# Moving half a chunk of matmuls and the search's constants in a one-core transformer kernel

## The chip, the cores and the metric

The kernel runs on one core of a Trainium2 chip. The metric is the device time of one execution in microseconds, the median of the runs.

## The reference, cut to what matters

`x` has two batch entries of 4096 tokens of width 256. Three stages follow one another: a tokenizer (linear attention with a 4096 x 4096 gate), an attention whose softmax runs over the two batch entries, and a feed-forward for the top half of the tokens, chosen by a router weight. The change touches the attention:

```python
h = tok(x)
mn = layernorm(layernorm(h)) * gamma + beta              # N = 2 entries, L = 4096 tokens
q, k, v = mn @ Wq, mn @ Wk, mn @ Wv                      # 8 heads of 32
g = sigmoid(mn @ Wg + bg)
att = softmax_t(sum over l, c of q[s] * k[t] * scale)    # a 2 x 2 table for each head
o = (sum over t of att[s, t, head] * v[t]) * g
h = h + o @ Wo + bo
h = h + ffn(top half of layernorm(h) by the router weight)
```

## The kernel before, in words

Five engines run instruction streams of their own, in order, and meet on semaphores. Matmuls of float32 data are made of three products of high and low halves (`split_products`). PSUM has eight banks of 128 x 512 float32.

- The tokenizer ends with the Gram sums (L713), which fill banks 0 to 3 in the last chunks.
- `start_mix` (L723) loads the attention's weights, and as soon as TensorE is past the Gram sums it runs the first half, j = 0, of chunk 0's values and gates: `values_and_gates(pr, pe, W2, M, 0, 0)`, 24 matmuls of 128x512 into banks 4 to 7 (V is banks 4 and 5, GB is banks 6 and 7). I write (c, j) for half j of chunk c, so this is (0, 0).
- `head_weights` (L814) makes the 2 x 2 tables. VectorE copies the Gram sums out of banks 0 to 3 (L856). TensorE multiplies them with Wk and Wq (L836, into banks 0 to 2) and VectorE multiplies the results elementwise (L860). TensorE forms the column sums (L845: 32 matmuls of 2 columns, into bank 3) and one more product (L849, into bank 3). Then VectorE and ScalarE make the softmax in small steps (L862 to L877), counted by `hw_step`. The last ones write `att_w`.
- `mix` (L886) walks over eight chunks of 512 tokens of both entries. For each half (c, j), ScalarE scales one value bank by `att_w` (`blend`, L976) and VectorE adds the other (`mixed`, L1020, semaphore `mx_o_ok`). ScalarE takes the sigmoid of the gate banks (L981, `mx_g_ok`), GpSimd multiplies (`gated`, L1120, `mx_og_ok`), ScalarE rounds (`high`, L988) and VectorE makes the low part (`low`, L1026, `mx_ogl_ok`). `project(c, h, s)` (L1158) then multiplies with Wo into banks 0 to 3. TensorE's order is (c, 0), project(c-1, 0), (c, 1), project(c-1, 1). ScalarE's order in chunk 0 is blend(0), high(0), blend(1), high(1), all in order.
- V and GB exist once, so (c, j) waits until the half before it is evacuated (L1177, L1182, L803).
- SyncE issues the loads in the order of the code: after the fourth product (`hw_tp`) the feed-forward's `w1`, `w2` and `b1` (L954 to L957), then chunk 1's four tiles of `halves` (`load_m`, L932, into the other half of a double buffer; semaphore `mx_m_ld1`), then the residual rows (L947).
- GpSimd, in `mix`, waits for `hw_step` 8 (the end of the head weights), then makes the constants for the feed-forward's top-k search (L1089 to L1106: `power`, `ones`, `before`, `index`, `step`, `grid`, `column`, `row`, `not_last`), and only then goes on to `gated`. `power` is first used by `scale` (L1129).

Of the kernel before, what the change touches and what calls it, by code (L numbers as in the profile page):

```python
# [722 lines left out]
def start_mix(pr, W2, heads_in, M, scratch, last_mnT):  # L723


    nc, ins, D, KD, END = pr.nc, pr.ins, pr.D, pr.KD, pr.B * pr.NC
    (ld, made, whi, wlo, m_ld) = (pr.sem(n) for n in ("hw_ld", "hw_made", "hw_hi", "hw_lo", "mx_m_ld0"))
    o_wr = pr.sem("hw_o_wr")
    head = D // pr.H
    block = pr.block  # L730

    @block.sync
    def _(sp):
        sp.wait_ge(pr.sem("ret_done"), END * pr.ST)
        for x in "vg":
            sp.dma_start(heads_in[x][:, :, :], ins[f"attn_W{x}"].rearrange("(k p) n -> p k n", p=P)).then_inc(ld, 16)
        for b in range(2):
            for x in ("hi", "lo"):
                sp.dma_start(M["m_" + x][:, 0, b].bitcast(F32), scratch["mT_" + x][b, 0]).then_inc(m_ld, 16)
        for x in "okq":  # L740
            sp.dma_start(heads_in[x][:, :, 0:D], ins[f"attn_W{x}"].rearrange("(k p) n -> p k n", p=P)).then_inc(ld, 16)
        with nc.allow_non_contiguous_dma(reason="a bias column, once"):
            sp.dma_start(W2["bg_col"][:, :], ins["attn_bg"].rearrange("(k p) -> p k", p=P)).then_inc(ld, 16)
        sp.dma_start(W2["br"][:, :], ins["ffn_br"].partition_broadcast(P)).then_inc(ld, 16)

        sp.wait_ge(pr.sem("mnT_lo_ok"), END * 2)
        for x, tile in zip(("hi", "lo"), last_mnT):
            sp.dma_start(scratch["mT_" + x][pr.B - 1, pr.NC - 1], tile).then_inc(pr.sem("st_mnT"), 16)
        for n, count in (("st_h", 16), ("st_mn", 16), ("st_mnT", 32)):
            sp.wait_ge(pr.sem(n), count * END)  # L750

    @block.gpsimd
    def _(pool):
        pool.wait_ge(pr.sem("ret_done"), END * pr.ST)
        nc.gpsimd.memset(heads_in["same_head"][:, :], 0.0).then_inc(made, 1)
        nc.gpsimd.memset(heads_in["ones"][:, :], 1.0).then_inc(made, 1)
        pool.wait_ge(made, 2)
        for h in range(P // head):
            r = slice(h * head, (h + 1) * head)
            nc.gpsimd.memset(heads_in["same_head"][r, r], 1.0).then_inc(made, 1)  # L760
        pool.wait_ge(made, 2 + P // head)
        pool.wait_ge(ld, 16 * 7)
        pool.wait_ge(pr.sem("wr_ld"), 16)
        for k in range(KD):
            nc.gpsimd.tensor_tensor(heads_in["o_wr"][:, k, :], heads_in["o"][:, k, 0:D], W2["wr"][:, :], ALU.mult).then_inc(o_wr, 1)
        pool.wait_ge(pr.sem("hw_o_sum"), 2)
        nc.gpsimd.tensor_copy(heads_in["o"][:, :, D + 1:D + 2], heads_in["o"][:, :, D:D + 1]).then_inc(o_wr, 1)
        nc.gpsimd.tensor_scalar(W2["sum_wr"][:, :], W2["sum_wr"][:, :], -1.0, None, ALU.mult).then_inc(o_wr, 1)

    @block.scalar  # L770
    def _(act):
        act.wait_ge(ld, 16 * 7)
        for x in "vgo":
            if x == "o":
                act.wait_ge(o_wr, KD + 1)
            nc.scalar.activation(W2[x + "_hi"][:, :, :], heads_in[x][:, :, :], ACT.Copy).then_inc(whi, 1)

    @block.vector
    def _(dve):
        nc.vector.tensor_reduce(W2["sum_wr"][:, :], W2["wr"][:, :], AX_X, ALU.add).then_inc(pr.sem("hw_o_sum"), 1)  # L780
        dve.wait_ge(o_wr, KD)
        nc.vector.tensor_reduce(heads_in["o"][:, :, D], heads_in["o_wr"][:, :, :], AX_X, ALU.add).then_inc(pr.sem("hw_o_sum"), 1)
        for n, x in enumerate("vgo"):
            dve.wait_ge(whi, n + 1)
            nc.vector.tensor_tensor(W2[x + "_lo"][:, :, :], heads_in[x][:, :, :], W2[x + "_hi"][:, :, :].bitcast(F32),
                                    ALU.subtract).then_inc(wlo, 1)

    @block.tensor
    def _(pe):
        pe.wait_ge(m_ld, 64)  # L790
        pe.wait_ge(wlo, 2)
        pe.wait_ge(pr.sem("h_ok"), END * 2)
        pe.wait_ge(pr.sem("mnT_lo_ok"), END * 2)
        values_and_gates(pr, pe, W2, M, 0, 0)


def values_and_gates(pr, pe, W2, M, h, j, gates_free=()):

    cols = slice(j * P, (j + 1) * P)
    vv, gg = pr.sem("mx_vv"), pr.sem("mx_gg")  # L800
    for w, bank, sem, b in (("v", M["V"][1], vv, 1), ("v", M["V"][0], vv, 0), ("g", M["GB"][0], gg, 0),
                            ("g", M["GB"][1], gg, 1)):
        if w == "g" and gates_free:  # L803
            past(pe, pr.sem("mx_g_ok"), gates_free[b])
        i = 0
        for k in range(pr.KD):
            for ww, x in split_products(W2[w + "_hi"][:, k, cols], W2[w + "_lo"][:, k, cols],
                                        M["m_hi"][:, h, b, k, :], M["m_lo"][:, h, b, k, :]):
                i += 1
                mm = pe.matmul(bank[:, :], ww, x, start=i == 1, stop=i == 3 * pr.KD)  # L810
        mm.then_inc(sem, 1)


def head_weights(pr, W2, heads_in, grams, banks):  # L814

    nc, D, KD, B = pr.nc, pr.D, pr.KD, pr.B
    head = D // pr.H
# [10 lines left out]
    def _(pe):  # L828
# [18 lines left out]
        mm.then_inc(col_ok, 1)  # L847
        pe.wait_ge(cols_sb, 1)
        pe.matmul(attp, heads_in["same_head"][:, :], cols[:, :], start=True, stop=True).then_inc(att_ok, 1)  # L849

    @block.vector
    def _(dve):
# [33 lines left out]
def mix(pr, W2, M, products, room, scratch, router, mlp_raw, W3):  # L886
# [1 line left out]

    nc, ins, D, KD, NC = pr.nc, pr.ins, pr.D, pr.KD, pr.NC
    with ExitStack() as ctx:  # L890
        m_hi, m_lo, V, GB = (M[n] for n in ("m_hi", "m_lo", "V", "GB"))
        h_in, rows = (room[n] for n in ("h_in", "rows"))
        base, late = sb(nc, ctx, "base", [P, 2, 2, TPC, D]), sb(nc, ctx, "late", [P, 8 * CH])
        og_hi, og_lo = (sb(nc, ctx, n, [P, 2, 2, KD, CH], F32R) for n in ("og_hi", "og_lo"))
# [66 lines left out]
        def _(act):  # L961
# [8 lines left out]

            def blend(c, j):
                n = c * 4 + 2 * j
                act.wait_ge(vv, n + 2)
                past(act, o_ok, n)
                for s in range(2):
                    nc.scalar.activation(t1[:, s, :], V[1][:, :], ACT.Copy,  # L976
                                         scale=W2["att"][:, s, 1, j:j + 1]).then_inc(t_ok, 1)
                past(act, og_ok, n)
                for s in range(2):
                    act.wait_ge(gg, n + s + 1)  # L980
                    nc.scalar.activation(g_sb[:, s, :], GB[s][:, :], ACT.Sigmoid,  # L981
                                         bias=W2["bg_col"][:, j:j + 1]).then_inc(g_ok, 1)
# [30 lines left out]
        @block.vector  # L1013
        def _(dve):
            def mixed(c, j):
                for s in range(2):
                    n = c * 4 + 2 * j + s
                    past(dve, og_ok, n - 1)
# [63 lines left out]

        @block.gpsimd
        def _(pool):
            pool.wait_ge(pr.sem("hw_step"), 8)
            for n in ("st_mn", "st_mnT"):
                pool.wait_ge(pr.sem(n), (32 if n == "st_mnT" else 16) * pr.B * NC)
            made = pr.sem("mw_made")
            nc.gpsimd.memset(power[:, :], -0.5).then_inc(power_ok, 1)  # L1089
            nc.gpsimd.memset(W3["ones"][:, :], 1.0).then_inc(made, 1)  # L1090
            pool.wait_ge(made, 1)

# [11 lines left out]
            nc.gpsimd.tensor_copy(W3["row"][:, :], W3["index"][:, P:P + 1]).then_inc(made, 1)  # L1104
            pool.wait_ge(made, 6 + 2 * STEPS)
            nc.gpsimd.tensor_scalar(W3["not_last"][:, :], W3["row"][:, :], float(P - 1), None, ALU.is_lt).then_inc(made, 1)  # L1106

            def spread_lanes(c):

# [47 lines left out]
        def _(pe):  # L1157
# [16 lines left out]
            def step(c, h):  # L1174
                if within(c) and c > 0:
                    pe.wait_ge(m_ld[h], c // 2 * 64 + 64)
                    past(pe, o_ok, c * 4)  # L1177
                    values_and_gates(pr, pe, W2, M, h, 0, (c * 4 - 1, c * 4))
                if within(c, 1):
                    project(c - 1, 1 - h, 0)  # L1180
                if within(c):
                    pe.wait_ge(o_ok, c * 4 + 2)  # L1182
                    values_and_gates(pr, pe, W2, M, h, 1, (c * 4 + 1, c * 4 + 2))
                if within(c, 1):
                    project(c - 1, 1 - h, 1)

# [430 lines left out]
def build(nc, ins, out, batches, tokens, width, heads, hidden):  # L1617
# [3 lines left out]
    with ExitStack() as ctx:  # L1621
# [36 lines left out]
                   "w1": work[:, n:2 * n].rearrange("p (k n) -> p k n", k=KD)}  # L1658
        with ExitStack() as phase:
            halves = sb(nc, phase, "halves", [P, 4 * KD * hidden], F32R)  # L1660
            M = {"V": banks[4:6], "GB": banks[6:8]}
            M["m_hi"], M["m_lo"] = (halves[:, i * 2 * n:(i + 1) * 2 * n].rearrange(
                "p (h b k t) -> p h b k t", h=2, b=2, k=KD) for i in range(2))
            W2["bg_col"], W2["att"] = sb(nc, phase, "bg_col", [P, KD]), sb(nc, phase, "att_w", [P, 2, 2, KD])
# [2 lines left out]
            with ExitStack() as heads_phase:  # L1667
# [3 lines left out]
                     ("att", [P, 2, 2, 2]), ("top", [P, 2, 2]), ("shifted", [P, 2, 2, 2]), ("expd", [P, 2, 2, 2]),  # L1671
                     ("total", [P, 2, 2]), ("inv", [P, 2, 2])])}
                start_mix(pr, W2, heads_in, M, scratch, pr.last_mnT)
                head_weights(pr, W2, heads_in, gram_view(work, width), banks[0:4])
            products = psum[:, 0:TPC * CH].rearrange("p (j n) -> p j n", j=TPC)
            mix(pr, W2, M, products, room, scratch, router, mlp_raw, W3)
        mlp(pr, W2, W3, ident, scratch, router)
# [38 lines left out]
```

## Time and profile before

| | us |
|---|---|
| median of 3 runs | 2070.14 (2069.56 to 2070.2) |
| the profiled execution | 2072.95 |
| its span | 2071.2 |
| TensorE busy | 1988.7 (96%) |
| VectorE, ScalarE, GpSimd busy | 1222.2, 675.0, 451.0 |

The profiled execution took 2072.95 us, of which 2071.2 are the span that the trace covers; the remaining 1.75 us lie around it. It is 2.81 us over the median of the other runs. All rows and all clock times below are of this execution, in us from the start of its span. A matmul's duration in a row is its latency. Neighbours overlap, so the pace of a stretch is read from the starts.

### The profile page before, as it was taken

To read this page: it belongs to the slowest core of one execution; us is meant where nothing else is said; L and a number is where in the kernel's file an instruction comes from. 1 tells how busy PE (TensorE), PEld (TensorE's weight loads), DVE (VectorE), ACT (ScalarE), POOL (GpSimd) and SP (SyncE) were. 2 spreads that over 40 slices of the span, in tenths; PEclk is the share of its full clock that TensorE was granted. 3 is DMA by queue.
4 is the path that set the end of the run, shared out by engine and by line. 5 is a ranking of instruction groups with operands and counts; after the bars stand their busy time and mean duration, and the time that the engine had idled before them with its cause. 6 is when DMAs were issued, how large, how long until landed. Compare 5 with 4: busy or idle time off the path is not lost.

```text
span 2071.2 us, 27479 instructions
## 1 busy us (share of the span) xinstructions
PE 1988.7 (96%) x9534; PEld 1646.7 (80%) x9534; DVE 1222.2 (59%) x2220; ACT 675.0 (33%) x1093; POOL 451.0 (22%) x578
## 2 busy tenths in 40 slices
PE   7999999999999999999999999999999989829998
PEld 6888888888888888888888888888887878718897
DVE  4656565665656556656565665656554358756553
ACT  4422222222222225422222222222222147524454
POOL 3302020202202023312020201202023057532342
PEclk9999999999999999999999999999999989959999
DMA  4232433334243333242433334243334469620110
GB/s 143 88 105 73 162 112 122 112 122 145 75 164 112 122 112 132 72 153 81 154 112 123 111 122 150 73 162 112 112 112 143 148 241 313 220 77 22 42 42 31
DMA packets 88114, 250.14 MB, mean 121 GB/s; under 512 B 11968, under 2 KB 32448, under 8 KB 88000
## 3 DMA queue, kind: packets, MB, share of 16 engines
q1 hardware_dynamic: 84928, 240.27, 34.5%
q0 software_dynamic: 3072, 8.44, 1.3%
q8 instruction: 61, 1.00, 0.2%
q14 instruction: 53, 0.43, 0.1%
HBM read 194.05 MB, written 54.62 MB: 120 GB/s over the span
## 4 chain that ended last, share of the span: by engine, by line
PE 90%; DVE 4%; issue 2%; ACT 2%; POOL 1%; DMA 0%; SPq 0%; DVEq 0%; ACTq 0%; POOLq 0%
PE bank L663 34%; PE bank L678 34%; PE bank L1568 4%; PE bank L810 4%; PE bank L1588 4%; PE bank L713 3%; PE bank L1169 2%; PE bank L635 1%; PE bank L609 1%; PE bank L619 1%; DVE kt L482 0%; DVE vf L493 0%; PE bank L648 0%; ACT work L380 0%; PE bank L836 0%
## 5 line engine op out<-in xcount | busy, mean ns | idle before, releaser
L678 PE MATMUL bank<-x_hi,kt 128*128 128x512 f32 x2048 | 724.0, 395 | 1.5 <-DVE work L519 1.4
L519 DVE SCALAR_TENSOR_TENSOR work<-bank,d_col,gate 128x512 f32<-128x512 f32 x512 | 383.8, 750 | 553.7 <-PE bank L678 544.7
L398 ACT ACTIVATE p_hi<-work 128x512 fp32r<-128x512 f32 x512 | 324.1, 633 | 1065.5 <-PE bank L663 1024.9
L678 PEld LDWEIGHTS bank<-x_hi,kt 128*128 128x128 f32 x2048 | 384.4, 188 | 90.4 <-DVE work L519 2.4
L663 PE MATMUL bank<-p_hi,v_hi 128*128 128x512 f32 x1024 | 407.0, 397 | 0.3 <-ACT yT L360 0.2
L663 PE MATMUL bank<-p_hi,v_lo 128*128 128x512 f32 x1024 | 404.2, 395 | 0.0
L663 PE MATMUL bank<-p_lo,v_hi 128*128 128x512 f32 x1024 | 403.4, 394 | 0.0
L678 PE MATMUL bank<-x_lo,kt 128*128 128x512 f32 x1024 | 401.0, 392 | 0.0
L507 DVE TENSOR_TENSOR p_lo<-work,p_hi 128x512 fp32r<-128x512 f32 x512 | 367.4, 718 | 29.3 <-ACT p_hi L398 29.2
L568 POOL TENSOR_SCALAR spread<-mv 128x4 f32<-128x4 f32 x16 | 4.9, 308 | 1125.4 <-DVE mv L451 1125.4
L663 PEld LDWEIGHTS bank<-p_hi,v_hi 128*128 128x128 f32 x1024 | 192.2, 188 | 50.6 <-DVE p_lo L507 5.3
L663 PEld LDWEIGHTS bank<-p_hi,v_lo 128*128 128x128 f32 x1024 | 192.3, 188 | 46.3
L663 PEld LDWEIGHTS bank<-p_lo,v_hi 128*128 128x128 f32 x1024 | 193.2, 189 | 44.7
L678 PEld LDWEIGHTS bank<-x_lo,kt 128*128 128x128 f32 x1024 | 192.3, 188 | 43.4
L1534 DVE TENSOR_TENSOR act_lo<-act,act_hi 128x512 fp32r<-128x512 f32 x64 | 59.2, 925 | 91.0 <-ACT act_hi L1472 90.8
L1568 PE MATMUL bank<-ffn,act_hi 128*128 128x256 f32 x512 | 97.4, 289 | 0.0
L1588 PE MATMUL bank<-fx_hi,ffn 128*128 128x512 f32 x256 | 92.5, 408 | 2.2 <-DVE fx_lo L1483 2.2
L1568 PEld LDWEIGHTS bank<-ffn,act_hi 128*128 128x128 f32 x512 | 84.2, 194 | 4.3 <-DVE act_lo L1534 0.2
L575 POOL TENSOR_TENSOR mn_sb<-mn_sb,gamma 128x256 f32<-128x256 f32 x64 | 55.2, 893 | 98.7 <-DVE mn_sb L456 98.7
L1568 PE MATMUL bank<-ffn,act_lo 128*128 128x256 f32 x256 | 73.6, 288 | 0.0
L713 PE MATMUL bank<-kt 128*128 128x256 f32 (+1 forms) x384 | 68.3, 339 | 2.2 <-DVE kt L544 2.2
L713 PEld LDWEIGHTS bank<-kt 128*128 128x128 f32 x384 | 59.2, 189 | 11.2 <-DVE kt L544 2.9
(226 smaller groups left out, 2271.7 us busy)
## 6 DMA issues: line engine op xcount, KB each, us to landing
gate<-in_gateT SPq DMA_DIRECT2D x256, 512.0 KB, 3.6
work<-in_xT SPq DMA_DIRECT2D x32, 512.0 KB, 4.7
scratch_rows<-rows SPq DMA_DIRECT2D x16, 518.0 KB, 4.0
scratch_h<-work SPq DMA_DIRECT2D x16, 512.0 KB, 3.0
scratch_mn<-mn_sb SPq DMA_DIRECT2D x16, 512.0 KB, 6.8
scratch_mT_hi<-mT_hi SPq DMA_DIRECT2D x16, 512.0 KB, 2.7
scratch_mT_lo<-mT_lo SPq DMA_DIRECT2D x16, 512.0 KB, 4.0
gate<-scratch_mn SPq DMA_DIRECT2D x16, 512.0 KB, 4.2
```

What stands on the lines that cost most here:

```text
L398: nc.scalar.activation(p_hi[:, i % 2, :], p32[:, i % RP, :], ACT.Copy).then_inc(hi_done, 1)
L507: nc.vector.tensor_tensor(p_lo[:, i % 2, :], p32[:, i % RP, :], p_hi[:, i % 2, :].bitcast(F32), ALU.subtract).then_inc(lo_done, 1)
L519: nc.vector.scalar_tensor_tensor(p32[:, i % RP, :], S[i % 2][:, :], d_col[:, i:i + 1], gate[:, g % RG, j, :], ALU.add, ALU.mult).then_inc( ...
L575: nc.gpsimd.tensor_tensor(mn_sb[:, j, :], mn_sb[:, j, :], W["gamma"][:, :], ALU.mult).then_inc(scaled, 1)
L663: mm = pe.matmul(Y[m][:, :], v, p, start=i == 0 and n == 0, stop=i == ST - 1 and n == 2)
L678: mm = pe.matmul(S[i % 2][:, :], w, x, start=n == 1, stop=n == 3 * KD)
L713: mm = pe.matmul(out, w, x, start=early(c, 1) and j == 0 and n == 0, stop=False, skip_group_check=True)
L810: mm = pe.matmul(bank[:, :], ww, x, start=i == 1, stop=i == 3 * pr.KD)
L1169: mm = pe.matmul(products[:, j, 0:D + 2], x, w, start=i == 0, stop=i == 3 * KD - 1)
L1534: nc.vector.tensor_tensor(a_lo[:, j % 2, :], act32[:, j % 2, :], a_hi[:, j % 2, :].bitcast(F32), ALU.subtract).then_inc(al_ok, 1)
L1568: mm = pe.matmul(YB[t // 2][:, (t % 2) * D:(t % 2 + 1) * D], a, w, start=j == 0 and t % 2 == 0 and n == 0, stop=j == FT - 1 and n == 2, sk ...
L1588: mm = pe.matmul(HB[j % 2][:, :], w, x, start=n == 1, stop=n == 3 * KD)
```

## The change

The second half of chunk 0, (0, 1), gets four banks of its own: V_first is banks 1 and 0, GB_first is banks 2 and 3, and `blend` and `mixed` read from there (`mix_banks`). TensorE runs it at the end of `head_weights`, right behind the column sums and the product of L849; the matmuls into bank 3 wait for `hw_step` 1, VectorE's copy of that bank. Chunk 0 drops out of TensorE's loop in `mix`. (1, 0), which goes to banks 4 to 7, now waits for `mx_o_ok` 2 and the gates 1 and 2 only, the evacuation of (0, 0).

GpSimd makes the search's constants once the Gram sums are done (`g_done`) and the tokenizer's stores have left, and waits for `hw_step` 8 behind them. `power` is set after that wait.

```diff
+def mix_banks(M, c, j):
+    return (M["V_first"], M["GB_first"]) if (c, j) == (0, 1) else (M["V"], M["GB"])
...
-def values_and_gates(pr, pe, W2, M, h, j, gates_free=()):
+def values_and_gates(pr, pe, W2, M, c, h, j, gates_free=()):
+    V, GB = mix_banks(M, c, j)
...
+    for w, bank, sem, b in (("v", V[1], vv, 1), ("v", V[0], vv, 0), ("g", GB[0], gg, 0), ("g", GB[1], gg, 1)):
+        if (c, j) == (0, 1) and w == "g" and b == 1:
+            pe.wait_ge(pr.sem("hw_step"), 1)
...
         pe.matmul(attp, heads_in["same_head"][:, :], cols[:, :], start=True, stop=True).then_inc(att_ok, 1)
+        values_and_gates(pr, pe, W2, M, 0, 0, 1)
...
         def _(pool):
-            pool.wait_ge(pr.sem("hw_step"), 8)
             for n in ("st_mn", "st_mnT"):
                 pool.wait_ge(pr.sem(n), (32 if n == "st_mnT" else 16) * pr.B * NC)
+            pool.wait_ge(pr.sem("g_done"), NC)
             made = pr.sem("mw_made")
-            nc.gpsimd.memset(power[:, :], -0.5).then_inc(power_ok, 1)
...
             nc.gpsimd.tensor_scalar(W3["not_last"][:, :], W3["row"][:, :], float(P - 1), None, ALU.is_lt).then_inc(made, 1)
+            pool.wait_ge(pr.sem("hw_step"), 8)
+            nc.gpsimd.memset(power[:, :], -0.5).then_inc(power_ok, 1)
...
                 if within(c) and c > 0:
                     pe.wait_ge(m_ld[h], c // 2 * 64 + 64)
-                    past(pe, o_ok, c * 4)
-                    values_and_gates(pr, pe, W2, M, h, 0, (c * 4 - 1, c * 4))
+                    if c == 1:
+                        pe.wait_ge(o_ok, 2)
+                        values_and_gates(pr, pe, W2, M, c, h, 0, (1, 2))
+                    else:
+                        pe.wait_ge(o_ok, c * 4)
+                        values_and_gates(pr, pe, W2, M, c, h, 0, (c * 4 - 1, c * 4))
...
-                if within(c):
+                if within(c) and c > 0:
                     pe.wait_ge(o_ok, c * 4 + 2)
...
+            M = {"V": banks[4:6], "GB": banks[6:8], "V_first": [banks[1], banks[0]], "GB_first": banks[2:4]}
```

## Rows read from the trace of the kernel before

**Rows 1.** The page: TensorE's busy time, and the last chain by engine.
```profile
PE 1988.7 (96%) x9534; PEld 1646.7 (80%) x9534; DVE 1222.2 (59%) x2220; ACT 675.0 (33%) x1093; POOL 451.0 (22%) x578
...
PE 90%; DVE 4%; issue 2%; ACT 2%; POOL 1%; DMA 0%; SPq 0%; DVEq 0%; ACTq 0%; POOLq 0%
```
**Rows 2.** Who waited for whom, TensorE: us in total, times, the longest.
```profile
PE bank L810 <- DVE late L1020: 7.6, 2, 4.0
```
**Rows 3.** Timeline, TensorE: start, length, instruction, idle before it and its releaser.
```profile
1645.02 0.63 PE L810 MATMUL bank<-halves,wv_hi 128*128 128x512 f32 x2
...
1650.62 1.89 PE L836 MATMUL bank<-hw_k,work 128*128 128x256 f32 x8
...
1662.33 0.61 PE L849 MATMUL bank<-hw_cols,hw_same_head 128*128 128x16 f32 x2 [0.27 <-DVE hw_cols L862]
1666.99 1.22 PE L810 MATMUL bank<-halves,wv_hi 128*128 128x512 f32 x2 [4.05 <-DVE late L1020]
...
1677.82 1.19 PE L810 MATMUL bank<-halves,wv_hi 128*128 128x512 f32 x2 [3.51 <-DVE late L1020]
...
1686.25 0.28 PE L1169 MATMUL bank<-wo_hi,og_hi 128*128 128x258 f32 x1
...
1689.11 0.62 PE L810 MATMUL bank<-halves,wv_hi 128*128 128x512 f32 x2
```
**Rows 4.** Stretches of this stage: length, busy times, granted clock, DMA share, GB/s.
```profile
1657.50:1662.30 4.80, 4.57 (x33) 4.46 (x31) 0.86 (x2) 0.00 (x0) 0.00 (x0) 0.76 0.65 232
1662.30:1667.00 4.70, 0.62 (x3) 0.51 (x3) 2.54 (x10) 2.49 (x4) 2.19 (x7) 0.50 1.10 330
1667.00:1670.40 3.40, 3.40 (x8) 2.71 (x9) 0.00 (x0) 1.53 (x3) 3.21 (x6) 0.52 1.02 412
1670.40:1674.20 3.80, 3.80 (x17) 2.82 (x15) 0.00 (x0) 0.48 (x1) 3.72 (x7) 1.00 0.78 312
...
1677.80:1683.50 5.70, 5.68 (x13) 4.44 (x14) 2.39 (x2) 1.55 (x4) 3.64 (x3) 0.50 1.00 400
1683.50:1686.20 2.70, 2.70 (x12) 2.19 (x11) 1.41 (x2) 1.77 (x3) 0.23 (x1) 0.92 0.08 30
```
**Rows 5.** Timeline, ScalarE, of the first chunk of the mix.
```profile
1664.70 1.26 ACT L976 ACTIVATE late<-bank,att_w 128x512 f32<-128x512 f32 x2 [0.85 <-DVE att_w L877]
...
1667.28 1.27 ACT L981 ACTIVATE late<-bank,bg_col 128x512 f32<-128x512 f32 x2
...
1675.50 1.25 ACT L976 ACTIVATE late<-bank,att_w 128x512 f32<-128x512 f32 x2
```
**Rows 6.** Timeline, GpSimd: constants from 1664.59 to 1672.4, then the gated products.
```profile
1664.59 0.11 POOL L1089 MEMSET power<- 128x4 f32 x1 [23.57 <-DVE att_w L877]
...
1672.21 0.23 POOL L1106 TENSOR_SCALAR not_last<-row 128x1 f32<-128x1 f32 x1
1672.40 2.53 POOL L1120 TENSOR_TENSOR late<-late 128x512 f32<-128x512 f32 x2
```
**Rows 7.** Timeline, VectorE: the Gram sums' copies, and chunk 0's second low parts.
```profile
1645.22 1.95 DVE L856 COPY work<-bank 128x512 f32<-128x512 f32 x4 [3.45 <-PE bank L713]
...
1679.45 2.54 DVE L1026 TENSOR_TENSOR og_lo<-late,og_hi 128x512 fp32r<-128x512 f32 x2 [1.78 <-ACT og_hi L988]
```
**Rows 8.** Timeline, SyncE's queue: the first and last of chunk 1's four loads.
```profile
1659.29 3.42 SPq L932 DMA_DIRECT2D halves<-scratch_mT_hi  x1
...
1663.97 0.48 SPq L932 DMA_DIRECT2D halves<-scratch_mT_lo  x1
```
**Rows 9.** DMA issues, of the last of these: size, us from issue to landing.
```profile
halves<-scratch_mT_lo SPq DMA_DIRECT2D x1, 512.0 KB, 7.7
```
**Rows 10.** Stretches elsewhere (columns of rows 4): tokenizer, and the feed-forward's first unit.
```profile
70.00:75.00 5.00, 4.24 (x18) 2.93 (x17) 4.93 (x8) 3.18 (x7) 4.09 (x8) 1.00 0.35 105
...
1860.00:1865.00 5.00, 2.88 (x10) 1.97 (x8) 4.49 (x8) 3.26 (x6) 2.85 (x2) 0.84 0.18 53
1865.00:1870.00 5.00, 4.35 (x17) 4.07 (x18) 2.55 (x9) 1.12 (x2) 0.00 (x0) 0.50 0.02 3
```

More of the change, by code:

```diff
@@ L793, in _ @@
         pe.wait_ge(pr.sem("mnT_lo_ok"), END * 2)
-        values_and_gates(pr, pe, W2, M, 0, 0)
-def values_and_gates(pr, pe, W2, M, h, j, gates_free=()):
+        values_and_gates(pr, pe, W2, M, 0, 0, 0)
+def mix_banks(M, c, j):
+    return (M["V_first"], M["GB_first"]) if (c, j) == (0, 1) else (M["V"], M["GB"])
+def values_and_gates(pr, pe, W2, M, c, h, j, gates_free=()):
+    V, GB = mix_banks(M, c, j)
     cols = slice(j * P, (j + 1) * P)
     vv, gg = pr.sem("mx_vv"), pr.sem("mx_gg")
-    for w, bank, sem, b in (("v", M["V"][1], vv, 1), ("v", M["V"][0], vv, 0), ("g", M["GB"][0], gg, 0),
-                            ("g", M["GB"][1], gg, 1)):
+    for w, bank, sem, b in (("v", V[1], vv, 1), ("v", V[0], vv, 0), ("g", GB[0], gg, 0), ("g", GB[1], gg, 1)):
+        if (c, j) == (0, 1) and w == "g" and b == 1:
+            pe.wait_ge(pr.sem("hw_step"), 1)
         if w == "g" and gates_free:
@@ L811, in values_and_gates, with head_weights @@
         mm.then_inc(sem, 1)
-def head_weights(pr, W2, heads_in, grams, banks):
+def head_weights(pr, W2, heads_in, grams, banks, M):
     nc, D, KD, B = pr.nc, pr.D, pr.KD, pr.B
@@ L890, in mix @@
     with ExitStack() as ctx:
-        m_hi, m_lo, V, GB = (M[n] for n in ("m_hi", "m_lo", "V", "GB"))
+        m_hi, m_lo = M["m_hi"], M["m_lo"]
         h_in, rows = (room[n] for n in ("h_in", "rows"))
@@ L972, in blend @@
                 n = c * 4 + 2 * j
+                V, GB = mix_banks(M, c, j)
                 act.wait_ge(vv, n + 2)
@@ L1015, in mixed @@
             def mixed(c, j):
+                V, _ = mix_banks(M, c, j)
                 for s in range(2):
@@ L1176, in step @@
                     pe.wait_ge(m_ld[h], c // 2 * 64 + 64)
-                    past(pe, o_ok, c * 4)
-                    values_and_gates(pr, pe, W2, M, h, 0, (c * 4 - 1, c * 4))
+                    if c == 1:
[4 more added lines that the diff above has]
+                        values_and_gates(pr, pe, W2, M, c, h, 0, (c * 4 - 1, c * 4))
                 if within(c, 1):
                     project(c - 1, 1 - h, 0)
-                if within(c):
+                if within(c) and c > 0:
                     pe.wait_ge(o_ok, c * 4 + 2)
-                    values_and_gates(pr, pe, W2, M, h, 1, (c * 4 + 1, c * 4 + 2))
+                    values_and_gates(pr, pe, W2, M, c, h, 1, (c * 4 + 1, c * 4 + 2))
                 if within(c, 1):
@@ L1660, in build @@
             halves = sb(nc, phase, "halves", [P, 4 * KD * hidden], F32R)
-            M = {"V": banks[4:6], "GB": banks[6:8]}
+            M = {"V": banks[4:6], "GB": banks[6:8], "V_first": [banks[1], banks[0]], "GB_first": banks[2:4]}
             M["m_hi"], M["m_lo"] = (halves[:, i * 2 * n:(i + 1) * 2 * n].rearrange(
@@ L1673, in build @@
                 start_mix(pr, W2, heads_in, M, scratch, pr.last_mnT)
-                head_weights(pr, W2, heads_in, gram_view(work, width), banks[0:4])
+                head_weights(pr, W2, heads_in, gram_view(work, width), banks[0:4], M)
             products = psum[:, 0:TPC * CH].rearrange("p (j n) -> p j n", j=TPC)
```

## The prediction

> **What bounds the kernel now.** I read the page first. TensorE is busy for 96% of the span, and the chain that ended last lies on it for 90% [rows 1]. A change can gain only where TensorE stands still or runs slowly, so I next asked for whom it waited. The reader should see two waits of the values and gates (L810) for the mix of the half before, 7.6 us together, the longest 4.0 [rows 2]. TensorE's timeline gives their places. After the head weights' last product, which ends at 1662.94, it idles 4.05 us and starts (0, 1) at 1666.99; it idles again for 3.51 us and starts (1, 0) at 1677.82. It reaches project(0, 0) at 1686.25, and from there on it does not stop in this stage [rows 3].
>
> The stretches show a second loss. The granted clock is 1.00 (2.4 GHz) up to the column sums, falls to 0.50 (1.2 GHz) while they run, and stays there until some 3.4 us into (0, 1). After the second idle time it is 0.50 once more, for 5.7 us of (1, 0) [rows 4]. (0, 0), the same 24 matmuls at full clock, took 1650.62 - 1645.02 = 5.60 us. (0, 1) took from 1666.99 to 1677.82 - 3.51 = 1674.31, which is 7.32 us, and (1, 0) took 1686.25 - 1677.82 = 8.43 us [rows 3].
>
> **The change, part by part.** The landmark is the start of project(0, 0), 1686.25 now. What lies before 1662.94 keeps its order on TensorE.
>
> (0, 1) starts at about 1662.95 instead of 1666.99. It no longer waits for the mix of (0, 0); what it adds is a wait for `hw_step` 1, VectorE's 0.2 us copy right behind the last product. That wait stands before the 19th matmul, so I cost it at nothing. If the copy were late, (1, 0) would queue behind it. The start falls into a stretch at 0.50, so I take the durations of the two halves that also started low: 7.32 us, or 8.43 us as the other end. (0, 1) then ends at 1670.3 or at 1671.4.
>
> (1, 0) is queued next. Its banks are free early: the mix of (0, 0) is done by 1666.9, when it releases TensorE now [rows 3], and the two sigmoids end at 1667.28 + 1.27 = 1668.55 [rows 5]. What is late next is the data. Chunk 1's loads stand in SyncE's queue behind the two big feed-forward weights. The last is issued at 1663.97 and lands 7.7 us later, at 1671.7 [rows 8, 9]. Before, there were 6 us of slack on it and nobody waited. Neither the order nor the release of these DMAs changes, since they wait for `hw_tp` alone. So (1, 0) starts at 1671.8 for either end of (0, 1), and a new idle time of 0.4 to 1.5 us stands before it.
>
> How long (1, 0) then takes is the largest unknown. The clock should have risen during (0, 1), as it did about 3.4 us after the earlier resume, and a short pause need not undo it. In the tokenizer a stretch with 0.76 us idle kept 1.00. In the feed-forward's first unit a stretch with 2.12 us idle was followed by one at 0.50 [rows 10]. The new pause lies between. I take 5.60 us, the full-clock row, because the pause is nearer to the first row for most of its range; the bound is 8.43 us, the whole of the slow row. (1, 0) ends at 1677.4, at worst at 1680.2.
>
> **GpSimd's part.** Chunk 0 of the mix is a chain in which ScalarE rounds (0, 0) before it blends (0, 1), and it can round only when GpSimd has multiplied. GpSimd does so at 1672.40, not because of the gate, ready at about 1667.95, but because its constants fill 1664.59 to 1672.4 [rows 5, 6]. After the change these 7.8 us lie behind the Gram sums, which VectorE begins to copy at 1645.22 [rows 7]; so they run from about 1645.3 to 1653.1, beside the copies and the elementwise products. If they doubled the copies' 1.95 us, these would end at 1649.1, still before the products at 1650.62 [rows 3, 7]: cover of 3.4 us, and I cost it at nothing. Setting `power` late costs 0.11 us, and its first reader comes after chunk 0.
>
> The multiplications then start at 1668.0, 4.4 us earlier, and the chain moves with them. The blend of (0, 1) moves from 1675.50 to 1671.1, after its value banks (first 12 of its matmuls, at most 12/24 of a low half of 10.3 us, so by 1668.1). The first low part of (0, 1), now ready at 1679.45 + 0.7 = 1680.1, is ready at 1675.7. Project(0, 0) needs this and TensorE's turn: it starts at max(1675.7, 1677.4) = 1677.4. Without GpSimd's part it would be 1680.1, so that part is worth up to 2.7 us.
>
> Behind it, (1, 1) wants to start 2.86 us later, at 1680.3 (1689.11 - 1686.25 [rows 3]), and needs the mix of (1, 0). ScalarE is free for that at 1676.3, and the mix takes about 2.2 us, from the blend's start at 1664.70 to 1666.9 [rows 3, 5], so it is ready between 1678.5 and 1679.2. One microsecond of slack is left, and TensorE is again the bound, as now. SyncE's load of chunk 2 is released by the gates of (0, 1), earlier too, and has until 1688.7.
>
> **The sum.** 1686.25 - 1677.4 = 8.85 us gained: 4.04 from (0, 1)'s earlier start, 3.51 - 0.1 from the second wait, 2.83 from the clock in (1, 0), less about 1.4 for the new wait for data. Everything behind is a chain on TensorE and the search, which should move as a block. The profiled time 2072.95 becomes 2064.1. It lies 2.81 over the median, and 2070.14 - 8.85 gives 2061.3.
>
> **A transfer that is slower.** In the sum the four tiles land at 1671.7 because the queues moved 412 GB/s from 1667.0 to 1670.4. The stretch before shows 330 [rows 4]. If the last 4.7 us of the transfer ran at that pace, 1.94 MB would take 5.9 us and land at 1672.9; (1, 0) would end at 1678.5, and the time would be 2062.5. Here the Trainium skill weighs against my number: its page "SBUF — State Buffer", section "Summary: rules for kernel authors", says to plan HBM loads at about 358 GB/s. By that figure the landing is an estimate of 1672.4 and the time 2062.0. The trace shows 412 sustained for such a load, and the measurement decides.
>
> **Rivals.**
> 1. The clock. The pause before (1, 0), or the slow start, leaves the clock at 0.50 for a good part of (1, 0). For it speaks the feed-forward's row; against it, the shortness of the pause. The price is up to 2.83 us: 2062.5 to 2064.1. Chance 0.22.
> 2. The late transfer, 2062.5 and somewhat more if the weights' traffic is in its way as well: chance 0.08.
> 3. The gain is larger. All that follows starts 8.85 us earlier, and the clock need not rise and fall at the same instructions. In the feed-forward's first unit it is low for about 6.6 us between 1860 and 1870 and a little after [rows 10]; without that fall up to 3.4 us more are saved. That gives 2058 to 2060.5. Chance 0.12.
> 4. The gain is given back in the mix or at its end, by a wait for stores or loads that had hidden behind the old pauses. I see none: chunk 2's loads get 17 us. It would give 2068 to 2072. Chance 0.04.
> 5. Slower, by one mechanism: the clock that fell in the column sums does not rise. At 1.2 GHz a half takes 10.3 us, so (0, 1) ends at 1673.2 and (1, 0) at 1683.5, still 2.8 us early. Project(0, 0) costs 2.3 more and (1, 1) 4.7 more, and at its end the kernel is 4.1 us behind: 2074.3. It decides from about 1688 on; TensorE would have to run low through 25 us of dense matmuls, where the longest such start seen here took 5.7 us [rows 4]. Chance 0.03.
> The rest, 0.51, is the forecast.
>
> **How the numbers follow.** About 0.2%, or 4.1 us, is what a measurement of this kernel can tell from no change. The forecast and rivals 1 to 3 all end faster than 2066.0: 0.93. Rival 4 is same, 0.04, and rival 5 slower, 0.03. The range takes in rivals 1 and 2 above and most of rival 3 below: 2058.5 to 2064.6.
>
> **What the profile would show.** TensorE should go from L849 into L810 with no idle time, at 1662.95, and wait once, up to 1.5 us, for a DMA of `halves` at about 1671.8. GpSimd's constants should lie at 1645 to 1653, its first L1120 near 1668.0, and project(0, 0) near 1677.4. The copies of L856 should end before 1650. The prediction is wrong if (1, 0) shows 0.50, if its data lands at another time, or if project(0, 0) waits for a low part after 1677.4.

## The result, and the profile after

The changed kernel takes 2065.94 us in the median, the kernel before 2071.07 us in the runs beside it; the ratio is 0.9974, with a 95% interval of 0.9965 to 0.9983. The interval leaves out 1: it is faster, by some 5.4 us (3.5 to 7.2). I had forecast 8.85 us and 2061.3, with a range up to 2064.6: the direction is right, the size and the range are not. One of the changed kernel's twelve executions took 4401.3 us, for a reason that nothing here shows, and the ratio leaves it out. Two further timings of the same kernel (e3 and e10 below) gave 0.9968 (0.9956 to 0.998) and 0.9967 (0.9955 to 0.9979), 6.6 and 6.8 us.

The profiled execution tells another story at first sight. Its span is 2062.0 us, 9.2 less than the 2071.2 of the one before. Lines have moved: L818 is now the values and gates (L810 before), L857 the last product of the head weights (L849), L1182 `project` (L1169), L1133 the gated product (L1120). This is TensorE's timeline, as in [rows 3]: start, length, instruction, idle time before it.

```profile
1645.27 0.63 PE L818 MATMUL bank<-halves,wv_hi 128*128 128x512 f32 x2
...
1661.97 0.61 PE L857 MATMUL bank<-hw_cols,hw_same_head 128*128 128x16 f32 x2 [0.27 <-DVE hw_cols L871]
1662.42 1.20 PE L818 MATMUL bank<-halves,wv_hi 128*128 128x512 f32 x2
...
1672.43 0.73 PE L818 MATMUL bank<-halves,wv_hi 128*128 128x512 f32 x2 [1.73 <-DMA halves<-scratch_mT_lo]
...
1678.13 0.28 PE L1182 MATMUL bank<-wo_hi,og_hi 128*128 128x258 f32 x1
```

The two waits for VectorE's share of the mix are gone. (0, 1) follows the last product without a pause, and one new wait of 1.73 us stands before (1, 0), for chunk 1's data. The stretches, as in [rows 4] (length, busy times by engine, granted clock, DMA share, GB/s):

```profile
1662.40:1667.60 5.20, 5.20 (x13) 4.13 (x14) 2.56 (x10) 3.43 (x6) 0.10 (x1) 0.50 1.09 336
1667.60:1672.40 4.80, 3.10 (x13) 2.12 (x11) 2.50 (x4) 3.28 (x7) 2.55 (x2) 0.98 1.02 410
1672.40:1678.10 5.70, 5.67 (x24) 4.60 (x25) 3.75 (x6) 3.89 (x7) 3.98 (x3) 1.00 1.03 410
```

The clock is 0.50 for the first 5.2 us of (0, 1), rises within it and holds over the pause, so (1, 0) takes 5.70 us. GpSimd's timeline, as in [rows 6]:

```profile
1645.59 0.21 POOL L1100 MEMSET ones<- 128x128 bf16 x1 [4.32 <-PE bank L713]
...
1653.18 0.23 POOL L1116 TENSOR_SCALAR not_last<-row 128x1 f32<-128x1 f32 x1
...
1667.76 2.55 POOL L1133 TENSOR_TENSOR late<-late 128x512 f32<-128x512 f32 x2 [3.43 <-ACT late L991]
```

The constants lie behind the Gram sums, and the first gated product starts at 1667.76 instead of 1672.40. On VectorE, as in [rows 7], the copies of the Gram sums take 1.95 us beside the constants, exactly as without them, and the low parts of (0, 1) start 4.6 us earlier:

```profile
1645.47 1.95 DVE L865 COPY work<-bank 128x512 f32<-128x512 f32 x4 [3.46 <-PE bank L713]
...
1674.86 2.54 DVE L1037 TENSOR_TENSOR og_lo<-late,og_hi 128x512 fp32r<-128x512 f32 x2 [1.80 <-ACT og_hi L998]
```

**A yardstick.** (0, 0) starts at 1645.02 in one profile and at 1645.27 in the other, and between 1644.41 and 1647.73 over all profiles of this study, though nothing ahead of it was changed. So I compare the stage, from the start of (0, 0) to the start of project(0, 0). It took 41.23 us before [rows 3] and takes 1678.13 - 1645.27 = 32.86 us: 8.4 us gained where the timing says 5 to 7. The experiments had to explain both what each half of the change does and where the 2 us went.

### The profile page after: what moved, and what is told of

It is laid out like the page before. It is cut to its first block, busy times and chain, and to the rows that moved or that the text cites. A ratio compares the mean times of both kernels' runs of the same rounds, so it can differ in the third digit from the quotient of the medians.

```text
span 2062.0 us, 27479 instructions
## 1 busy us (share of the span) xinstructions
PE 1985.3 (96%) x9534; PEld 1643.8 (80%) x9534; DVE 1222.6 (59%) x2220; ACT 675.0 (33%) x1093; POOL 453.0 (22%) x578
## 4 chain that ended last, share of the span: by engine, by line
PE 92%; DVE 3%; issue 2%; DMA 1%; ACT 1%; SPq 1%; POOL 0%; DVEq 0%; ACTq 0%; POOLq 0%
PE bank L663 35%; PE bank L678 34%; PE bank L1585 4%; PE bank L818 4%; PE bank L1605 4%; PE bank L713 3%; PE bank L1182 2%; PE bank L635 2%; PE bank L648 1%; PE bank L619 1%; PE bank L609 1%; DMA halves<-scratch_mT_lo 0%; PE bank L844 0%; PE bank L1574 0%; DVE top_counts L1278 0%
## 5 line engine op out<-in xcount | busy, mean ns | idle before, releaser
L519 DVE SCALAR_TENSOR_TENSOR work<-bank,d_col,gate 128x512 f32<-128x512 f32 x512 | 383.9, 750 | 553.4 <-PE bank L678 544.0
```

The source lines that it names most:

```text
L519: nc.vector.scalar_tensor_tensor(p32[:, i % RP, :], S[i % 2][:, :], d_col[:, i:i + 1], gate[:, g % RG, j, :], ALU.add, ALU.mult).then_inc( ...
```

## The experiments

Where a ratio is given, the kernel was timed beside the kernel before; e4, e7, e8 and e12 are one profiled execution each. The diffs are against the kernel named. A gain in us is the ratio's distance from 1, taken of the median before; the stage is that of the one profile.

**e1, GpSimd's half alone** (against the kernel before):

```diff
         def _(pool):
-            pool.wait_ge(pr.sem("hw_step"), 8)
...
+            pool.wait_ge(pr.sem("g_done"), NC)
             made = pr.sem("mw_made")
-            nc.gpsimd.memset(power[:, :], -0.5).then_inc(power_ok, 1)
...
+            pool.wait_ge(pr.sem("hw_step"), 8)
+            nc.gpsimd.memset(power[:, :], -0.5).then_inc(power_ok, 1)
```

> GpSimd's half of the change alone: the constants are made behind the Gram sums, the second half of chunk 0 stays in the shared banks and in its old place. Theory A (the stage works as I costed it): (0, 1) still starts at 1667, but the multiplications start 4.4 us earlier, the wait before (1, 0) shrinks from 3.5 us to nothing, (1, 0) starts at about 1674.3 and runs at full clock, 5.6 us: project(0, 0) at about 1679.9 and some 6 us gained, more than the whole change gained in the timed runs (5.1). Theory B (in ordinary runs the clock is high anyway, and the profiled execution of before was an unlucky one): only the 3.5 us of waiting go, about 3.5 us gained or less.

Measured: 2065.61 us, ratio 0.9976 (0.9965 to 0.9986), 5 us. The stage took 33.60 us. TensorE waits for the mix only once in it (timeline):

```profile
1665.82 1.22 PE L810 MATMUL bank<-halves,wv_hi 128*128 128x512 f32 x2 [4.05 <-DVE late L1020]
...
1672.97 0.63 PE L810 MATMUL bank<-halves,wv_hi 128*128 128x512 f32 x2
...
1678.57 0.28 PE L1170 MATMUL bank<-wo_hi,og_hi 128*128 128x258 f32 x1
```

(0, 1) takes 7.15 us, and (1, 0) follows with no pause and takes 5.60. The interval, 2.9 to 7.2 us, holds both theory A's 6 us and theory B's 3.5; the profile decides between them, and it shows A's course. The 4.4 us by which GpSimd is earlier clear the second wait and the clock loss behind it. Of theory B, one half comes back below: the first profile of the kernel before was an unlucky one.

**e2, the banks' half alone** (against the changed kernel: GpSimd's edit above undone).

> The banks' half alone: (0, 1) runs behind the column sums in banks of its own, the constants stay where they were. By the working of the prediction project(0, 0) then waits for the low part of (0, 1), ready at 1680.1: 6.1 us gained against before, 2 us behind the whole change. If instead the data of chunk 1 sets the end of this stage, it is as fast as the whole change (project(0, 0) near 1678).

Measured: 2066.54 us, ratio 0.9978 (0.9969 to 0.9987), 4.6 us. The stage took 34.47 us. TensorE's wait for chunk 1's data, and the row of project(0, 0):

```profile
PE bank L818 <- DMA halves<-scratch_mT_lo: 2.8, 1, 2.8
```

```profile
1682.20 0.39 PE L1180 MATMUL bank<-wo_hi,og_hi 128*128 128x258 f32 x1 [0.24 <-DVE og_lo L1037]
```

So that project did wait for its low part, as I had worked out. The idle time is short, 0.24 us, only because (1, 0) ended late as well: it waited 2.79 us for its data, and behind this pause it took 7.41 us. An earlier (1, 0) would have gained nothing: the low part's instruction started at 1681.05 and took 1.10 us, to 1682.15, that is 34.4 us behind (0, 0), where I had worked out 35.1. In this version GpSimd's late constants set the end of the stage. Against the changed kernel beside it (e3) it is 2.9 us slower in the median and 1.7 us in the stage; I had expected 2. Either half of the change alone gains most of what both gain.

**e3 and e4, both kernels again**, unaltered.

> The changed kernel unaltered, for a second profiled execution and more timed runs on the chip of the others. Theory A (the gain in the stage is 8 us in every execution, and part of it is lost elsewhere): from the start of (0, 0) to project(0, 0) it takes 32.9 us as in the first profile, and the rest of the span varies. Theory B (the stage itself differs from run to run with the clock): this stretch is 1.5 to 3 us longer. Timed: 0.9974 of before again, 5 us.

> The kernel before, unaltered, for a second profiled execution. Theory A: from (0, 0) to project(0, 0) 41.2 us again, span within 2 us of 2071.2. Theory B: in this stretch the clock comes back earlier or does not fall before (1, 0), and it takes 38.5 to 40 us, a span near 2068.

Measured: the changed kernel 2063.68 us, ratio 0.9968 (0.9956 to 0.998), its stage 32.78 us, as e3's theory A has it (e10 below will differ). The kernel before gave 2071.03 us with a span of 2069.3, and its stage took 39.50 us instead of 41.23: (1, 0) took 7.20 us instead of 8.43, and the way from (0, 0) to (0, 1) 0.5 us less. The distance from (0, 1) to (1, 0), 10.84 us, is unchanged; what moved is when the clock came back. The start of (1, 0) in its timeline:

```profile
1678.17 0.89 PE L810 MATMUL bank<-halves,wv_hi 128*128 128x512 f32 x2 [3.02 <-DVE late L1020]
```

**e7, e8 and e12, the kernel before three more times**, to learn how the first profile stands among others.

> The kernel before, unaltered, for a third profiled execution. The first two took 41.23 and 39.50 us from (0, 0) to project(0, 0), with a mean granted clock of 0.977 and 0.978. Theory B: with a mean clock of 0.981 this stretch is 38 to 38.7 us (the 2.8 us of (1, 0) are not lost at all); with 0.977 to 0.978 it is 39.5 to 41.3. Theory A: 39.5 to 41.3 with any mean clock.

> As the run before this one: a fourth profiled execution of the kernel before, with the same two expectations.

> A fifth profiled execution of the kernel before. The four so far took 41.23, 39.50, 39.63 and 38.71 us from (0, 0) to project(0, 0), with 8.43, 7.20, 7.22 and 7.02 us for (1, 0). If the first was the exception: 38.7 to 39.7 us again.

| kernel before | stage | (0, 0) to (0, 1) | (0, 1) to (1, 0) | (1, 0) | behind it |
|---|---|---|---|---|---|
| first profile | 41.23 | 21.97 | 10.83 | 8.43 | 384.95 |
| e4 | 39.50 | 21.46 | 10.84 | 7.20 | 383.93 |
| e7 | 39.63 | 21.58 | 10.83 | 7.22 | 383.74 |
| e8 | 38.71 | 20.86 | 10.83 | 7.02 | 383.48 |
| e12 | 38.91 | 20.85 | 10.84 | 7.22 | 383.77 |

The first profile was the exception, as e12's text has it: it is the longest in every column that varies at all. The mean stage is 39.60 us. Theory A, 39.5 us or more in every execution, falls with e8 and e12. Theory B is right that the loss differs between executions (its 38 to 38.7 us met 38.71 and 38.91) and wrong on how: it expected no clock loss in (1, 0) in the good ones, and all five show one. Their shortest (1, 0), 7.02 us, is still 1.4 over the full-clock 5.6. The other varying column is the way to (0, 1), and there the column sums. In e8 the clock held through them and fell only in the pause behind; the stretches of e8:

```profile
1656.90:1661.20 4.30, 4.03 (x35) 3.84 (x33) 0.87 (x2) 0.00 (x0) 0.00 (x0) 1.00 0.68 224
1661.20:1665.20 4.00, 0.01 (x1) 0.00 (x0) 2.54 (x10) 2.42 (x4) 2.12 (x7) 0.60 1.10 319
...
1676.10:1679.00 2.90, 2.90 (x7) 2.32 (x8) 1.12 (x2) 1.34 (x3) 2.90 (x3) 0.50 1.01 386
1679.00:1683.10 4.10, 4.10 (x18) 3.32 (x18) 2.68 (x3) 1.96 (x3) 0.97 (x2) 0.99 0.78 313
```

In e8 the low level lasts 2.9 us into (1, 0), where the first profile has 5.7 [rows 4].

**e6, the clock held up in the second pause** (against the kernel before; 14 matmuls more, whose result nobody reads):

```diff
                     pe.wait_ge(m_ld[h], c // 2 * 64 + 64)
+                    if c == 1:
+                        for i in range(14):
+                            pe.matmul(products[:, 0, :], W2["v_hi"][:, 0, 0:P], m_hi[:, 1, 0, 0, :], start=True, stop=True)
                     past(pe, o_ok, c * 4)
```

> The kernel before, with 14 additional matmuls of 512 columns, whose result nobody reads, in TensorE's pause before (1, 0); the waits stay. Theory B (the kernel before loses a different amount in each execution because the clock falls in this pause in some and not in others): (1, 0) takes 5.6 us in every execution, the median falls by 1 to 2.8 us below 2070.9 and the slowest executions (2072 to 2074) are gone. Theory A (the stage is the same in every execution, and the clock costs the same 2.8 us each time): 2.8 us or more gained in all executions, the spread stays. If the clock does not matter: no change, or slower by what the matmuls run over the end of the pause.

Measured: 2068.69 us beside 2071.3, ratio 0.9989 (0.998 to 0.9998). The runs spread over 3.8 us (2067.01 to 2070.78); those of before over 5.3 (2069.33 to 2074.64). The stretches of the pause and of (1, 0):

```profile
1674.30:1677.80 3.50, 3.44 (x15) 2.45 (x14) 3.15 (x4) 2.89 (x6) 0.94 (x2) 1.00 0.66 227
1677.80:1683.50 5.70, 5.70 (x24) 4.60 (x25) 3.72 (x4) 3.38 (x6) 4.01 (x4) 1.00 1.02 407
```

With the waits left in place and TensorE kept busy, the clock stays at 1.00 and (1, 0) takes 5.70 us, 1.7 less than the mean of the five profiles (7.42). The median gained is 2.3 us with an interval of 0.4 to 4.1. So the clock in (1, 0) was worth about 1.7 us in an ordinary execution, not the 2.83 of my sum. The two profiles that reached (0, 1) as early as this one, e8 and e12 (20.86 and 20.85 us, here 20.85), put it at 1.3 to 1.5. That the slowest runs are gone fits a price that varies with it, but eleven runs do not prove it.

**e5 and e11, chunk 1's data earlier** (against the changed kernel):

```diff
             def step(c, h):
-                if within(c, -1):
+                if within(c, -1) and c > 0:
                     load_m(c + 1, 1 - h)
...
+            sp.wait_ge(pr.sem("g_done"), NC)
+            load_m(1, 1)
             sp.wait_ge(pr.sem("hw_tp"), 4)
             sp.dma_start(mlp_raw["w1"], ins["ffn_w1"].rearrange("(k p) n -> p k n", p=P)).then_inc(raw_ld, 16)
```

> The changed kernel with chunk 1's four loads issued as soon as the Gram sums are done (about 1645.5) instead of behind the feed-forward's weights (1659.5). Theory A (the new wait of 1.7 us for this data is on the path): (1, 0) starts where (0, 1) ends, 1670.7, ends at 1676.3, and project(0, 0) starts there, 0.8 us behind its low part: 1.7 us faster than the changed kernel, from (0, 0) to project(0, 0) about 31.1 us. Rival (another wait stands right behind, or the clock falls less often with the pause gone or more often): under 0.7 us.

> The changed kernel with early loads, again, beside the changed kernel on one chip: 31.1 us from (0, 0) to project(0, 0), and 1.7 us faster than the changed kernel; ratio to before 0.9955 to 0.9963.

Measured: 2062.65 us, ratio 0.9952 (0.9939 to 0.9966), and 2062.69 us, ratio 0.9957 (0.9943 to 0.997); beside e11 the changed kernel (e10) took 2064.79. The stage takes 31.09 and 31.54 us. This is the fastest version, 8.9 to 9.9 us under the kernel before. Of TensorE's waits in this stage e5 keeps only the 0.3 us for VectorE's copy of the column sums, which every version has; e11 has this one besides:

```profile
PE bank L1184 <- DVE og_lo L1039: 0.5, 1, 0.5
```

Between e11 and the changed kernel beside it lie 2.1 us in the median. The mean stages, 31.3 us here and 33.24 over the three profiles of the changed kernel, differ by 1.9, where 1.7 was expected. The wait for data was on the path. Now e11's project(0, 0) waits 0.5 us for its low part, so the evacuation through ScalarE and GpSimd is the next bound.

**e9, GpSimd's half with early data, without the banks** (both edits shown above, on the kernel before).

> GpSimd's half of the change with chunk 1's loads issued behind the Gram sums, without the banks' half. Theory C (without the banks (1, 0) starts only when (0, 1) ends, after its data has landed, so the loads are not on the path): from (0, 0) to project(0, 0) 33.6 us as in GpSimd's half alone, same time within 1 us. The banks are then worth 0.8 us with late data and 2.5 us with early data. Rival: the loads matter here too (they take the traffic off the first chunk's evacuation), 1 us or more faster than GpSimd's half alone.

Measured: 2065.76 us, ratio 0.9973 (0.9962 to 0.9985), as e1. The stage took 34.75 us, 1.15 more than e1's, but all of that lies ahead of (0, 1), in the column sums (22.15 us from (0, 0) to (0, 1), where e1 had 20.85). From (0, 1) to project(0, 0) it is 12.60 us, and 12.75 in e1. So theory C holds: without the banks the loads are not on the path. With the data early, the banks are worth 3.1 us in the median (e11's 2062.69, timed beside this 2065.76).

**e10, the changed kernel a third time.**

> The changed kernel unaltered, on the chip and against the runs of the others of this call. From (0, 0) to project(0, 0) 32.8 us; if the gain of the stage is 7 us in the mean, the ratio lies at 0.9966 to 0.9971. If the first timing (0.9974, 5 us) is the truth, 2 us of the stage's gain are lost elsewhere and it comes out there again.

Measured: 2064.79 us, ratio 0.9967 (0.9955 to 0.9979). But the stage took 34.08 us instead of the 32.8 expected, and this profile shows rival 1 at work. The wait for the data (2.81 us here, as (0, 1) had run faster) and the stretches of (0, 1), of the pause and of the start of (1, 0):

```profile
1674.15 0.73 PE L818 MATMUL bank<-halves,wv_hi 128*128 128x512 f32 x2 [2.81 <-DMA halves<-scratch_mT_lo]
```

```profile
1663.90:1671.30 7.40, 7.40 (x26) 5.63 (x25) 2.58 (x11) 4.66 (x7) 2.10 (x3) 0.77 1.06 353
1671.30:1674.10 2.80, 0.04 (x1) 0.00 (x0) 2.65 (x4) 2.24 (x4) 0.53 (x1) 1.00 1.02 411
1674.10:1677.50 3.40, 3.35 (x9) 2.65 (x10) 1.57 (x2) 1.88 (x4) 3.11 (x3) 0.62 1.03 407
```

Here the clock was still 1.00 through the pause and fell soon after (1, 0) had started; (1, 0) took 7.24 us. A faster (0, 1) did not help: it only made the pause longer. In e2 as well the pause was 2.8 us and the clock fell behind it, and in the two profiles with 1.7 us it held. That the length of the pause decides is the likely reading, but it is not shown: in e2 and e10 the clock had also run full through the column sums and fallen only in (0, 1), and no run parts the two. The mean stage of the changed kernel over three profiles (32.86, 32.78, 34.08) is 33.24 us.

## Why the prediction was wrong in size

The mean stage is 39.60 us before and 33.24 after: 6.4 us, in line with the three timings (5.4, 6.6 and 6.8). My 8.85 splits into this and two errors, 1.6 on the stage before and 0.9 on the stage after.

**The step that failed is the sum**, "1686.25 - 1677.4 = 8.85 us gained", and within it "2.83 from the clock in (1, 0)". I priced the removed stage by the one profiled execution and took the result off the median of other runs. The text itself says that this execution lay 2.81 over the median, and did not ask where the excess lay. The five profiled executions show where: 41.23 - 39.60 = 1.6 us lay in the very stage that the change shortens, 1.0 of it in (1, 0), which is 7.42 us in the mean, and 0.6 in the column sums, which the change doesn't touch. Behind the stage lay another 1.0. A gain taken from this execution belongs under its own time, and against the median it should have been about 7.2 us. The two profiled executions do differ by 9.2 us, so the pair of profiles seemed to confirm the sum while the timed runs did not. A smaller part of the miss is no matter of the gain: the sum started from 2070.14, the median of three runs, and twelve runs beside the changed kernel gave 2071.07.

**The stage after** was forecast at 1677.4 - 1645.02 = 32.4 us and is 33.24 in the mean, 0.9 more. In the first profile the last load was issued at 1664.03 and landed 8.4 us later, at 1672.4, not at 1671.7: with the two starts set off against each other this is some 0.5 us, the rival of the slower transfer in small. In the mean of the three profiles (1, 0) starts 27.03 us behind (0, 0), 0.25 later than forecast. The Trainium skill's figure of about 358 GB/s ("SBUF — State Buffer", "Summary: rules for kernel authors") is not what made it late; the traffic ran at 410 GB/s once more, and the 336 before it are as [rows 4] have them. What did change is the neighbour: SyncE now issues chunk 2's loads from 1670.73, before this landing, and before the change from 1674.34, after it. That they took from its pace is not shown. The larger rest, 0.61 us of the mean, is the clock, rival 1, which came in one profile of three: (1, 0) took 5.70, 5.70 and 7.24 us, where I had 5.60.

**Right, point by point.** (0, 1) at 1662.42 behind the last product, with no wait for `hw_step` 1; its length 8.3 us, near the upper of my two values (7.32 and 8.43); the new wait for the four tiles, its place and in two profiles nearly its length (1.73 and 1.68 us, 2.81 in the third, forecast 0.4 to 1.5); the clock held over it in two profiles of three; the constants at 1645.6 to 1653.4 and at no cost to the copies; the low part of (0, 1) ready at 1674.86 + 1.10 = 1675.96, which is as far behind (0, 0) as the forecast 1675.7, but by luck: the 0.7 us that I gave the instruction are 1.1 in both kernels, and it started that much sooner than I had it. Rival 2 of the smaller kind (late data) came, rival 1 in part. Rival 3, a gain in the feed-forward, is not seen: behind project(0, 0) it took 383.0 to 383.9 us in the three profiles of the changed kernel and 383.5 to 385.0 before, where 3.4 us were at stake. Rivals 4 and 5 did not come.

**Too low: GpSimd's part, "worth up to 2.7 us".** That was its worth once the banks are there. Alone it gained 5 us of time, and the stage of its one profile is 6.0 us under the mean of before. The banks add 33.60 - 33.24, some 0.4 us in the stage, or 0.9 if e9, which differs from e1 only in loads that are not on its path, is taken in (the mean of the two is 34.2). It is no more because with them (1, 0) runs into the wait for data: it starts 27.0 us after (0, 0) in the mean of the three profiles of the changed kernel (27.16, 27.08 and 26.84), and 28.0 us after it in e1. Timed side by side, the banks were worth 1.9 us (e1 and e3) and 1.0 us (e9 and e10). With the data early, banks and all give 31.3 us (mean of e5 and e11), and without the banks early data give nothing (e9). These last differences are of one to three profiles each and uncertain by half a microsecond.

## What to carry to other kernels

Before pricing a stall from one profile, compare that execution with the median of the runs, and where it is longer, ask whether the excess lies in the stage that you are about to change; a second profile of the kernel before would have shown most of it (39.50 us against 41.23). Two edits that shorten the same wait are not additive: work out each alone and both together, down to what is late next. When TensorE's work moves forward, look at when its data is issued: here a load put 14 us earlier in an idle queue was worth another 1.7 us, and a faster (0, 1) without it only lengthened the pause for the data.

## What the runs showed of the hardware

- The same kernel lost differing amounts to the granted clock at the same place. (1, 0), behind the same pause of 3.0 to 3.5 us, took 7.02 to 8.43 us in five profiles, and the way from (0, 0) to (0, 1), with the column sums in it, 20.85 to 21.97 us. Nothing in the kernel differed.
- Useless matmuls in a pause paid for themselves: 14 of them kept the clock at 1.00 and took 2.3 us off the median (interval 0.4 to 4.1).
- A pause of 1.7 us left the clock at 1.00 in two profiles; after pauses of 2.8 us (e2, e10) the next 24 matmuls took 7.41 and 7.24 us.
- GpSimd's constants beside VectorE's copies out of PSUM cost them nothing: 1.95 us with and without. VectorE's low parts are another case: of the four of chunk 0 in the changed kernel's first profile, the one that started with GpSimd at rest took 0.69 us, the three that met a multiplication or a cast of GpSimd 1.10, 1.10 and 1.30 us; the kernel before shows 0.69, 1.09, 1.09 and 1.29.
